# Mixing stage of a fused convolution block: an eight-block ring for h, and another division of the nine depthwise taps

## What is computed

```
h  = haar_dwt(group_norm(x))                  # 4 x 128 channels, 128 x 128 points
h  = gelu(batchnorm(conv1x1(h, w_c1)))        # back to 128 channels;  res = h
o  = dwconv3x3(h, dw_w)                       # nine taps, each channel by itself, zero padding
o  = layernorm over channel, row and column of one image
o  = conv1x1(gelu(conv1x1(o, pw1_w)), pw2_w)
h  = o + res                                  # "u" in the kernel
x  = x + haar_idwt(gelu(batchnorm(conv1x1(h, w_c2))))
out = x + blur4x4(group_norm(x))
```

## Time and profile before

| | |
|---|---|
| median of 3 runs | 5658.86 us (5644.84 to 5668.61) |
| the profiled execution's own time | 5669.07 us |
| its span | 5667.0 us |
| PE busy | 5208.1 us (92%) |
| DVE busy | 4342.4 us (77%) |
| ACT busy | 3725.1 us (66%) |
| POOL busy | 2141.6 us (38%) |
| granted PE clock, mean | 0.968 of full |
| mixing stage | from about 1239 to about 2587 us of the span |

### The profile page before, as it was taken

The page is one execution under the profiler, slowest core; times in us unless marked ns, Lnnn a source line. Parts: engine busy times, 40 slices in busy tenths (PEclk is TensorE's granted clock), DMA queues, the critical chain, the costliest instruction groups (busy, mean ns, idle before and its releaser), DMA issues. The chain is left out here.

```text
span 5667.0 us, 67162 instructions
## 1 busy us (share of the span) xinstructions
PE 5208.1 (92%) x18136; PEld 3155.5 (56%) x18136; DVE 4342.4 (77%) x5293; ACT 3725.1 (66%) x5012; POOL 2141.6 (38%) x1429
## 2 busy tenths in 40 slices
PE   2888888886999999997699999999999999999999
PEld 1333333332555555563256666666666666666777
DVE  8555555418999999966888888888888888888833
ACT  1333333346787777755678787787887878878744
POOL 0000000018777777732333433333333333333354
PEclk9999999998999999998899999999999999999999
DMA  9999999842333333326999999999999999999986
GB/s 369 379 382 373 375 375 366 351 142 71 107 110 107 105 107 108 107 86 240 336 388 401 396 401 398 390 402 387 400 392 379 394 388 399 398 391 390 399 292 228
DMA packets 829594, 1729.83 MB, mean 305 GB/s; under 512 B 50064, under 2 KB 587152, under 8 KB 718608
## 3 DMA queue, kind: packets, MB, share of 16 engines
q1 hardware_dynamic: 755472, 1389.81, 67.2%
q10 hardware_dynamic: 73728, 335.58, 14.4%
HBM read 1050.95 MB, written 674.23 MB: 304 GB/s over the span
## 5 line engine op out<-in xcount | busy, mean ns | idle before, releaser
L1115 POOL TENSOR_TENSOR y_lo<-y_centred_tile,y_hi 128x1024 fp32r<-128x1024 f32 x512 | 1040.0, 2052 | 1727.9 <-ACT y_centred_tile L1457 1413.8
L1336 PE MATMUL blur_psum<-y_hi,band_hi 128*128 128x512 f32 x4096 | 1127.8, 417 | 8.8 <-DVE y_tile L1204 7.4
L1319 PE MATMUL conv_psum<-u_in,w_conv 128*128 128x512 f32 x2048 | 977.0, 621 | 100.5 <-DMA u_in<-u_scratch 69.0
L1336 PE MATMUL blur_psum<-y_lo,band_hi 128*128 128x512 f32 x4096 | 1041.9, 396 | 7.5 <-POOL y_lo L1115 7.1
L1336 PEld LDWEIGHTS blur_psum<-y_hi,band_hi 128*128 128x128 f32 x4096 | 764.9, 188 | 278.7 <-issue 100.7
L1336 PEld LDWEIGHTS blur_psum<-y_lo,band_hi 128*128 128x128 f32 x4096 | 769.4, 188 | 200.7 <-POOL y_lo L1115 16.5
L1176 DVE TENSOR_TENSOR pair_sums<-gelu_out,conv_psum 128x512 f32<-128x512 f32 x960 | 614.2, 684 | 308.7 <-ACT conv_psum L1427 308.6
L1427 ACT ACTIVATE gelu_out<-conv_psum,bn_shift,bn_scale 128x512 f32<-128x512 f32 x512 | 398.1, 777 | 555.8 <-PE conv_psum L1319 532.6
L1204 DVE SCALAR_TENSOR_TENSOR y_tile<-blur_psum,rstd_all,y_tile 128x1024 f32<-128x1024 f32 x512 | 639.6, 1277 | 159.5 <-PE blur_psum L1336 152.2
L1319 PEld LDWEIGHTS conv_psum<-u_in,w_conv 128*128 128x128 f32 x2048 | 401.2, 199 | 553.0 <-issue 412.9
L608 POOL TENSOR_TENSOR tap_products<-tap_products 128x512 f32<-128x512 f32 x512 | 653.4, 1276 | 43.3 <-ACT tap_products L869 6.7
(11 more groups left out here) (172 smaller groups left out, 5643.9 us busy)
## 6 DMA issues: line engine op xcount, KB each, us to landing
x_tile<-x SPq DMA_DIRECT2D x256, 1024.0 KB, 10.0
y_scratch<-x_tile ACTq DMA_DIRECT2D x256, 1024.0 KB, 8.5
y_tile<-y_scratch SPq DMA_DIRECT2D x512, 512.0 KB, 10.9
out<-y_tile SPq DMA_DIRECT2D x512, 512.0 KB, 10.4
x_stream<-x SPq DMA_DIRECT2D x192, 1024.0 KB, 11.3
x_resident<-x SPq DMA_DIRECT2D x160, 1024.0 KB, 11.2
z_scratch<-z_tile ACTq DMA_DIRECT2D x256, 256.0 KB, 7.1
z_in<-z_scratch SPq DMA_DIRECT2D x256, 256.0 KB, 3.0
```

The costliest lines, as they stand in the source:

```text
L1115: nc.gpsimd.tensor_tensor(y_lo[:, h, part, 2:2 + W], y_c[:, part, :], y_hi[:, h, part, 2:2 + W].bitcast(F32), ALU.subtract).then_inc(s_lo, 1)
L1319: nc.tensor.matmul(cv[s][:], w[:, s * C:(s + 1) * C], u_t[:, k % US, :], start=True, stop=True).then_inc(s_mm, 1)
L1336: ins = nc.tensor.matmul(bl[t][:, 2 * c:2 * c + 2, :], wt[:, kw, :], y[:, h, ch:ch + 2, kw:kw + W], start=(m == 0 and kw == 0), stop=(m == ...
```

## The change

The ring is cut from 41 to 8 blocks. A place is free when the depthwise of the step that reads it last is complete (`s_oo`) and the h in it is stored: SP now stores each h block over its z in HBM after `gelu_first`, and loads it back into one of four `h_in` slots, issued three positions ahead of the residual, which reads `h_in` in place of the ring. The store of u is issued one position later.

The nine taps are no longer divided as 2 (PE), 4 (DVE), 3 (ACT and POOL). The first 36 steps take 4, 3, 2. After that even steps take 2, 4, 3 and odd steps 1, 4, 4. POOL makes as many additions in a step as ACT makes products. `products` becomes a ring of 12 single slots, each freed by the addition that reads it. The edge rows at the ring's seam are now written once in 8 blocks, not once in 41.

```diff
-PE_TAPS = 2
-ACT_TAPS = 3
-DVE_TAPS = TAPS - PE_TAPS - ACT_TAPS
+ENTER_TAPS = (4, 3, 2)
+STEADY_TAPS = ((2, 4, 3), (1, 4, 4))
+PE_MOST = 4
+PR_SLOTS = 12
-BLOCKS = STEPS + 1 + BEHIND + 1
+BLOCKS = 8
+H_SLOTS = 4
+def split_of(e):
+    return ENTER_TAPS if e < LEAVE - LAG_DW else STEADY_TAPS[e % 2]
...
-        products = sb("tap_products", [128, 2, ACT_TAPS, BANK])
+        products = sb("tap_products", [128, PR_SLOTS, BANK])
...
+        def last_reader(at):
+            b, j = divmod(at, STEPS + 1)
+            return b * STEPS + min(j + 1, STEPS - 1) if j < STEPS else min((b + 1) * STEPS, ALL2 - 1)
+        def wait_place(engine, at):
+            if at == BLOCKS - 1:
+                engine.wait_ge(s_oo, 1)
+            if at < BLOCKS:
+                return
+            engine.wait_ge(s_oo, last_reader(at - BLOCKS) + 1)
             b, j = divmod(at - BLOCKS, STEPS + 1)
-            return b * STEPS + min(j, STEPS - 1)
+            if j < STEPS:
+                e = b * STEPS + j
+                engine.wait_ge(s_hst[e % 8], 16 * (e // 8 + 1))
...
+            def store_h(e):
+                sp.wait_ge(s_h, e + 1)
+                b, j = divmod(e, STEPS)
+                sp.dma_start(zv[b, :, j * BANK:(j + 1) * BANK].rearrange("c (r w) -> c r w", w=W2),
+                             rows_of(e)).then_inc(s_hst[e % 8], 16)
+            def load_h(l):
+                if l >= H_SLOTS:
+                    sp.wait_ge(s_u, l - H_SLOTS + 1)
+                sp.wait_ge(s_hst[l % 8], 16 * (l // 8 + 1))
+                b, j = divmod(l, STEPS)
+                sp.dma_start(h_in[:, l % H_SLOTS, :], zv[b, :, j * BANK:(j + 1) * BANK]).then_inc(s_hin[l % H_SLOTS], 16)
...
-            for p in range(-AHEAD, ALL2 + LEAVE):
+            for p in range(-AHEAD, ALL2 + LEAVE + 1):
...
-                if p >= LEAVE:
-                    store(p - LEAVE)
+                if 0 <= p - 1 < ALL2:
+                    store_h(p - 1)
+                if 0 <= p + 3 - LEAVE < ALL2:
+                    load_h(p + 3 - LEAVE)
+                if p - 1 >= LEAVE:
+                    store(p - 1 - LEAVE)
...
-                pr = products[:, e % 2]
-                for n in range(1, ACT_TAPS):
-                    pool.wait_ge(s_pr, e * ACT_TAPS + n + 1)
+                first = products[:, ACT_BEFORE[e] % PR_SLOTS, :]
+                for n in range(1, split_of(e)[2]):
+                    pool.wait_ge(s_pr, ACT_BEFORE[e] + n + 1)
                     if n > 1:
-                        pool.wait_ge(s_add, e * (ACT_TAPS - 1) + n - 1)
-                    nc.gpsimd.tensor_tensor(pr[:, 0, :], pr[:, 0, :], pr[:, n, :], ALU.add).then_inc(s_add, 1)
+                        pool.wait_ge(s_add, ADD_BEFORE[e] + n - 1)
+                    nc.gpsimd.tensor_tensor(first, first, products[:, (ACT_BEFORE[e] + n) % PR_SLOTS, :],
+                                            ALU.add).then_inc(s_add, 1)
...
                 dve.wait_ge(s_p2, l + 1)
+                dve.wait_ge(s_hin[l % H_SLOTS], 16 * (l // H_SLOTS + 1))
...
-                    rows_of(l), ALU.add, ALU.add).then_inc(s_u, 1)
+                nc.vector.scalar_tensor_tensor(u_t[:, l % 4, :], p2_p[:], V[:, V_PW2B:V_PW2B + 1],
+                                               h_in[:, l % H_SLOTS, :], ALU.add, ALU.add).then_inc(s_u, 1)
...
-                if e >= 2:
-                    act.wait_ge(s_oo, e - 1)
-                for n in range(ACT_TAPS):
-                    k = TAPS - ACT_TAPS + n
+                for n in range(split_of(e)[2]):
+                    i = ACT_BEFORE[e] + n
+                    if i >= PR_SLOTS:
+                        e0, n0 = PRODUCTS[i - PR_SLOTS]
+                        if n0 == 0:
+                            act.wait_ge(s_oo, e0 + 1)
+                        else:
+                            act.wait_ge(s_add, ADD_BEFORE[e0] + n0)
```

More of the change, by code:

```diff
@@ L439 @@
 Z_SLOTS = 3
+DVE_BEFORE = [0]
+ACT_BEFORE = [0]
+ADD_BEFORE = [0]
+for step in range(ALL2):
+    DVE_BEFORE.append(DVE_BEFORE[-1] + split_of(step)[1])
+    ACT_BEFORE.append(ACT_BEFORE[-1] + split_of(step)[2])
+    ADD_BEFORE.append(ADD_BEFORE[-1] + split_of(step)[2] - 1)
+PRODUCTS = [(e, n) for e in range(ALL2) for n in range(split_of(e)[2])]
 def phase_mix(nc, kp, pw1, pw2, const, z_d, u_d):
@@ L450, in phase_mix @@
         plane = sb("h_ring", [128, 4 * BLOCKS + 2, W2 + 2])
+        h_in = sb("h_in", [128, H_SLOTS, BANK])
         o_buf = sb("depthwise_out", [128, O_SLOTS, BANK])
         z_in = sb("z_in", [128, Z_SLOTS, BANK])
-        diag = sb("tap_diagonals", [128, PE_TAPS, C])
+        diag = sb("tap_diagonals", [128, PE_MOST, C])
         w1 = sb("pw1_weights", [128, C])
@@ L469, in phase_mix @@
         KR = kp["KR"]
-        band = products[:, 0, 0, :].rearrange("p (k m) -> p k m", m=128)
-        sband = products[0:96, 0, 1, 0:192].rearrange("p (k m) -> p k m", m=48)
+        band = products[:, 0, :].rearrange("p (k m) -> p k m", m=128)
+        sband = products[0:96, 1, 0:192].rearrange("p (k m) -> p k m", m=48)
         dw_p = [ps(f"dw_psum{i}", [128, BANK]) for i in range(2)]
@@ L490, in phase_mix @@
         s_h = sem("h_rows_ready")
+        s_hst = [sem(f"h_stored{i}") for i in range(8)]
+        s_hin = [sem(f"h_loaded{i}") for i in range(H_SLOTS)]
         s_dw = sem("dw_psum_ready")
@@ L582, in gap @@
                 at = b * (STEPS + 1) + STEPS
-                last = freed_by(at)
-                if last is not None:
-                    pool.wait_ge(s_u, last + 1)
+                wait_place(pool, at)
                 r = 1 + at % BLOCKS * R2
@@ L588, in gap @@
                     pool.memset(plane[:, 4 * BLOCKS + 1, :], 0.0)
+                if at % BLOCKS == BLOCKS - 1:
+                    pool.memset(plane[:, 0, :], 0.0)
                 pool.memset(plane[:, r:r + R2, :], 0.0).then_inc(s_fill, 1)
@@ L633, in _ @@
             dve.wait_ge(s_id, 16)
-            for k in range(PE_TAPS):
+            for k in range(PE_MOST):
                 nc.vector.tensor_scalar(diag[:, k, :], K[:, K_ID:K_ID + C], V[:, V_DWW + k:V_DWW + k + 1],
@@ L654, in depthwise @@
                 acc = dw_p[e % 2][:]
-                for n, k in enumerate(range(PE_TAPS, PE_TAPS + DVE_TAPS)):
-                    to = o_buf[:, e % O_SLOTS, :] if n == DVE_TAPS - 1 else acc
+                on_pe, on_dve, _ = split_of(e)
+                for n, k in enumerate(range(on_pe, on_pe + on_dve)):
+                    to = o_buf[:, e % O_SLOTS, :] if n == on_dve - 1 else acc
                     taps.link(nc.vector.scalar_tensor_tensor(
@@ L750, in _ @@
         def _(pe):
-            pe.wait_ge(s_bn1, 1 + PE_TAPS)
+            pe.wait_ge(s_bn1, 1 + PE_MOST)
             pe.wait_ge(s_zero, 5)
@@ L758, in taps_step @@
                 if e >= 2:
-                    pe.wait_ge(s_lk_tap, (e - 1) * DVE_TAPS)
-                for k in range(PE_TAPS):
+                    pe.wait_ge(s_lk_tap, DVE_BEFORE[e - 1])
+                count = split_of(e)[0]
+                for k in range(count):
                     ins = nc.tensor.matmul(dw_p[e % 2][:], diag[:, k, :], tap(k, e),
-                                           start=(k == 0), stop=(k == PE_TAPS - 1))
+                                           start=(k == 0), stop=(k == count - 1))
                 ins.then_inc(s_dw, 1)
@@ L830, in gelu_first @@
                 at = block_of(e)
-                last = freed_by(at)
-                if last is not None:
-                    act.wait_ge(s_u, last + 1)
+                wait_place(act, at)
                 rows = z_in[:, e % Z_SLOTS, :].rearrange("p (r c) -> p r c", c=W2)
@@ L863, in tap_products @@
                 wait_rows(act, e)
-                if e >= 2:
-                    act.wait_ge(s_oo, e - 1)
-                for n in range(ACT_TAPS):
-                    k = TAPS - ACT_TAPS + n
-                    nc.scalar.activation(products[:, e % 2, n, :].rearrange("p (r c) -> p r c", c=W2), tap(k, e),
+                for n in range(split_of(e)[2]):
[6 more added lines that the diff above has]
+                            act.wait_ge(s_add, ADD_BEFORE[e0] + n0)
+                    k = TAPS - split_of(e)[2] + n
+                    nc.scalar.activation(products[:, i % PR_SLOTS, :].rearrange("p (r c) -> p r c", c=W2), tap(k, e),
                                          ACT.Copy, scale=V[:, V_DWW + k:V_DWW + k + 1]).then_inc(s_pr, 1)
```

11 lines of the change are left out of this document (3 added, 8 removed).

## The result

The changed kernel takes 5618.17 us (median of 6 runs, 5608.03 to 5625.56) against 5658.98 for the kernel before (6 runs). The ratio is 0.9935, with a 95% interval of 0.9921 to 0.9948: faster by 29 to 45 us. Run again beside eleven runs of the kernel before it took 5621.3 against 5653.34, ratio 0.9943 [0.9929, 0.9957]. The prediction was 5630 us, and 29 us faster.

The account below looks back on a forecast made before the run. PE was to bound filling and POOL steady running. Gains of 16.7 us (filling) and 12.5 us (steady part with changes of batch) made 29.2, so 5658.9 became 5629.7 us; the forecast's own range was 5615 to 5642.

Parts of the forecast that it names:

- Filling: First 36 steps of mixing: bound moves from POOL to PE, 3.99 to 3.43 us a step, gaining 16.7 us.
- the first step at half clock: Start of filling: two more PE taps at half clock make the first step about 2 us later.
- Steady step: Mixing after filling: POOL becomes the bound at 4.00 and 5.42 us in turn, mean 4.71 against 4.76.
- Rival B: Steady mixing: DVE at 4.50 us is the bound, not POOL; another 46 us less, 5584 us; chance 0.08.
- Changes of batch: Six changes between images in steady mixing: POOL's waits cost 4.3 us each, 26 us in all.
- The rule that the prediction cited: Changes of batch: VectorE instructions with two SBUF inputs contend with GpSimd reading SBUF, single-input ones do not; changes stay 4.3 us.
- DVE at 4.50: Steady mixing: DVE's own work stays 4.50 us a step, 0.2 us under POOL's 4.71.
- rival A: Steady step stays at 4.76 us through a wait between DVE, ACT and POOL; 5639 to 5655 us; chance 0.26.
- Reload costs nothing: Storing and reloading h, two more 256 KB DMAs a step: DMA share 0.66, no cost.
- The slots are slack: Inside a batch: 12 product slots let ACT run about three steps ahead, so no other engine should stop POOL.
- Draining moves with the sum: End of mixing: same instructions, PE the bound, its start hanging on POOL's end; no change in its length.
- rival C: Steady mixing: PE's clock falls, 3.95 us lost a step at half clock; 5709 us at 20 steps; chance 0.06.

Follow-up runs that it names:

- the old filling: Changed kernel with its first 36 steps divided 2, 4, 3 instead of 4, 3, 2: 5638.53 us, ratio 0.9977 to the kernel before.
- the almost free addition: Changed kernel with the fourth product added in only 2 of 512 columns: 5556.43 us, ratio 0.9829 to the kernel before.
- one in three: Changed kernel with taps 1, 4, 4 in every third steady step instead of every second: 5589.69 us, ratio 0.9887 to the kernel before.
- lighter steps after a change of batch: Changed kernel with 1, 4, 4 every third steady step, and each image's step 1 divided 4, 3, 2 and step 2 divided 3, 3, 3: 5574.99 us.
- old taps: Changed kernel with taps 2, 4, 3 in every step, keeping small ring, reload and 12 slots: 5654.94 us, ratio 1.0004 to the kernel before.
- seven slots: Changed kernel with 7 product and 34 depthwise output slots: 5695.99 us; same slots with the 41-block ring and no reload: 5695.5 us.

## Why the prediction was right, step by step

**Filling**: POOL to PE, 3.99 us a step to 3.43, as forecast, and shown by the run with the old filling. I had put 2 us for the first step at half clock; from the start of mixing to L612/L661 of step 0 the five traces of kernels whose first step is 2, 4, 3 show 13.5 to 14.3 us (mean 13.9), the eight with 4, 3, 2 show 14.5 to 16.2 (mean 15.5), so 1.6 us is the mean for it, though the first pair shows only 0.1. From DVE's end of step 32 to L612/L661 of step 36 I took 3 us off 25.9; it was 23.3, so 2.6. The clock was not quite full there, as I had it: 0.90 from 1358 to 1375.

**Steady step**: POOL's 4.00 and 5.42 were measured as 4.01 and 5.43, and the steady part as 1060.6 us against 1060.7 in the sum. That it agrees to 0.1 us is luck: the 110 odd and 109 even steps without their waits add up to 1033.3 us and not 1031.5, the changes of batch to 23.7 and not 26, the memsets to 3.4 and not 3.2. That POOL is the bound was shown by the almost free addition (66 us less) and by one in three. Rival B is out as well: two additions still span 2.70 us and three 4.12, so the gap of 0.15 us between them is still there.

**Changes of batch**: I had 4.3 us each, with POOL's wait for L600 and for the folded weights. After, at the third change:

```profile
1668.46 0.76 DVE L722 TENSOR_TENSOR small_columns<-o_mean_var,vectors 128x1 f32<-128x1 f32 x1
...
1669.26 1.31 DVE L723 SCALAR_TENSOR_TENSOR small_columns<-small_columns,o_mean_var 128x1 f32<-128x1 f32 x1
1669.29 1.26 POOL L661 TENSOR_TENSOR depthwise_out<-depthwise_out,tap_products 128x512 f32<-128x512 f32 x1
...
1672.44 4.09 POOL L656 TENSOR_TENSOR tap_products<-tap_products 128x512 f32<-128x512 f32 x3
...
1675.30 1.31 DVE L739 TENSOR_SCALAR pw_folded<-pw_weights,small_columns 128x128 f32<-128x128 f32 x1
...
1676.61 1.27 POOL L661 TENSOR_TENSOR depthwise_out<-depthwise_out,tap_products 128x512 f32<-128x512 f32 x1
```

L661 of steps 96 and 97, the first two of the image, are 7.32 apart where the bare step is 5.42, and the next is 6.02 later where it is 4.00, so 3.9 us in all. L722, L723 and L739 take 0.76, 1.31 and 1.31 us, to the end of POOL's addition each time; in the draining part, when POOL does not add, they take 0.16, 0.22 and 0.29. The rule that the prediction cited from the Trainium skill (SBUF — State Buffer, "Who interferes with whom") agrees with the first two, which have two inputs in SBUF. The same section of the Trainium skill names tensor_scalar among the operations that can take the shared ports, and L739 is one: the trace agrees, with 1.31 us against 0.29.

**DVE at 4.50**: the mis-sized term. It is 4.40 to 4.41 when DVE never waits. It changed no part of the sum, since POOL was above either, but it made the margin to POOL 0.3 us, not 0.2, and rival A less near than I had it.

**Reload costs nothing**: right, by two independent pairs (old taps, seven slots). The DMA share of 0.73 or 0.74 was nearer to 1 than the 0.66 that I had. The four transfers of a step, KB each and us from issue to landing:

```profile
u_scratch<-u_tile SPq DMA_DIRECT2D x20, 256.0 KB, 4.7
z_in<-z_scratch SPq DMA_DIRECT2D x20, 256.0 KB, 3.4
z_scratch<-h_ring SPq DMA_DIRECT2D x20, 256.0 KB, 3.9
h_in<-z_scratch SPq DMA_DIRECT2D x19, 256.0 KB, 4.5
```

A u store lands 4.7 us after issue, where it took 2.2 in the same window of the kernel before; it has three positions, 14 us, so nothing waits for it.

**The slots are slack**: right at 12 and, inside a batch, at 9. The run with 7 and the smaller depthwise output shows how little such a sentence may be trusted. The way from a freed slot to the addition I had put at 9.5 us; with 7 slots the loop shows about 10.1 for two steps, the wait for a depthwise output slot included. Of rival A the mechanism is real, and enough slots, of the products and of the depthwise output, keep it away.

**Draining moves with the sum**: wrong by 2.8 us. PE, ahead of POOL now, stands idle for the last statistics and loses its clock:

```profile
2445.38 0.50 PEld L861 LDWEIGHTS small<-small_columns,mean_over_channels 128*128 128x128 f32 x2 [4.53 <-DVE small_columns L723]
...
2446.72 1.93 PE L846 MATMUL gram_psum<-u_transposed 128*128 128x129 f32 x8
...
2448.43 1.91 PE L820 MATMUL pw_psum<-gelu_out,pw_weights 128*128 128x512 f32 x2
...
2450.14 1.82 PE L827 MATMUL pw_psum<-depthwise_out,pw_folded 128*128 128x512 f32 x2
...
2454.17 1.02 PE L827 MATMUL pw_psum<-depthwise_out,pw_folded 128*128 128x512 f32 x2
```

`gram`, `pw2` and `pw1` take 1.93, 1.91 and 1.82 us there, at the lower of TensorE's two clocks (1.2 GHz; the mean granted clock from 2443 to 2452 is 0.62), where they take 1.06 and 1.02 at full clock (2.4 GHz). In the kernel before, the first `pw1` of the last image started 5.0 us after the last addition, here 7.1. That is rival C in small. In the three traces with alternating taps and 12 slots (both of the changed kernel and the old filling) PE is idle 3.7 us before this group, the clock falls, and the part takes 111.8 to 112.3 us. In the ten others PE is idle 1.3 us or less there, the clock stays, and it is 109.6 each time. In the steady part of the changed kernel a lower clock was seen only at changes of batch, but at all six of them, 0.74 to 0.76 over some 13 us around each; in the profile of the kernel before it was 1.00 at four of the six. So the granted clock of the window above, with one of them in it, is 0.98.

**What stays open.** Mixing explains 28 us, and the other two stages, which the change does not touch, show 24 us more in the first pair of traces. The stage ahead was between 1227 and 1245 us over 13 traces, without order. The stage behind was 3080.0, 3072.2 and 3067.4 in three traces of the kernel before and 3060.6 and 3058.6 in two of the changed one, but 3055.6 to 3078.0 in the eight others, 3078.0 and 3055.6 both with the same ring and reload. Mixing's 28 us lie just under the first interval of the gain (29 to 45 us) and inside the second (24 to 40). For the nine other medians of several runs, the changed kernel's second among them, the total moved against the kernel before by what mixing moved, within some 4 us, and by 8 us more in one (lighter steps after a change of batch). So most of the 13 us that the first comparison shows beyond mixing looks like the spread of the runs, and the 12 us by which it beat the forecast with it; whether a few us are real and lie in the last stage was not settled.

## What to carry to other kernels

A bound engine relieved by 0.43 us a step gave 0.05, because the work went to the engine that was third in line; price each engine's step with the moved work, dependent gaps included (1.42, not 1.27, for an addition), and choose the mix at which several are equal, here one odd step in three. A change that looks like pure cost, storing and reloading 256 KB a step, can be worth it for the SBUF that it frees: with the 7 product slots and 34 output slots that were put beside the large ring, the new division is slower than the old. At a change of phase the dependent chain, not the mean, sets the time, and steps there may be divided otherwise.

## What the runs showed of the hardware that was not expected

VectorE's six instructions of a step take 4.40 us when none of them waits. When the residual waits for PE, right behind the statistics, they take 4.50 plus the wait; when the statistics wait for POOL, it is 4.38 plus the wait (1604.60 to 1609.62 in the changed kernel, 0.64 of it waiting). Statistics to residual is 0.60 us start to start without a wait, though the statistics instruction is 0.69 long, so these two overlap by about 0.1 us, and a wait between them takes that back.
